# Clearing a 177 MB scratch table by 3 large DMAs instead of 88 small ones, in a four-layer GNN kernel

## The reference

```python
h = jnp.maximum(_layernorm(x), 0.0)
x = x + _L0_gnn_ref(h, edge_index, ...)      # edge MLP, segment_max over dst
h = jnp.maximum(_layernorm(x), 0.0)
x = x + _L1_gnn_ref(h, src, dst, ...)        # GCN: segment_sum with degree norms
h = jnp.maximum(_layernorm(x), 0.0)
x = x + _L2_gnn_ref(h, ..., src, dst)        # two hops of mean aggregation
h = jnp.maximum(_layernorm(x), 0.0)
x = x + _L3_gnn_ref(h, edge_index, edge_weight, ...)
# L3: message = x[dst] * edge_weight; segment_sum(message, src); two products with weights
```

## Time and profile before

| | |
|---|---|
| median of 3 runs | 14147.0 us (14146.95 to 14180.07) |
| the profiled execution's own time | 14180.07 us |
| its span | 14178.3 us |
| PE busy | 7232.4 us, 51% |
| DVE busy | 9168.8 us, 65% |
| ACT busy | 5831.1 us, 41% |
| POOL busy | 7818.9 us, 55% |
| moved by DMA | 1969.50 MB, mean 139 GB/s |
| mean granted clock of PE | 0.71 |

### The profile page before, as it was taken

One profiled execution on the slowest core, in us unless ns is written; L12 is line 12 of the kernel. 1 busy time (PEld: TensorE's weight loads), 2 busy tenths in 40 slices (PEclk: granted clock), 3 DMA queues, 4 the chain that ended last, 5 costly groups with the idle time before them and its releaser, 6 DMA issues. The chain is left out here.

```text
span 14178.3 us, 285510 instructions
## 1 busy us (share of the span) xinstructions
PE 7232.4 (51%) x96792; PEld 5249.9 (37%) x96792; DVE 9168.8 (65%) x18447; ACT 5831.1 (41%) x10200; POOL 7818.9 (55%) x7194
## 2 busy tenths in 40 slices
PE   2266666666666655996999999400000000000356
PEld 1255555555555543554555555300000000000355
DVE  5388888888888885335333433565666666666575
ACT  0144444444444444774776677322222222222000
POOL 5677777777777753110111111577777777777200
PEclk9866667666666667997999899655555555555676
DMA  7333333333333335884787688322222222221585
GB/s 311 130 116 113 110 118 112 114 115 110 113 116 110 116 105 151 256 253 142 246 258 227 189 252 258 101 65 63 65 65 65 65 65 62 65 62 60 178 255 179
DMA packets 1268462, 1969.50 MB, mean 139 GB/s; under 512 B 256937, under 2 KB 987918, under 8 KB 1262785
## 3 DMA queue, kind: packets, MB, share of 16 engines
q1 hardware_dynamic: 861601, 1047.59, 24.1%
q10 hardware_dynamic: 174288, 612.09, 11.6%
q0 software_dynamic: 231664, 297.80, 7.9%
HBM read 1155.02 MB, written 815.55 MB: 139 GB/s over the span
## 5 line engine op out<-in xcount | busy, mean ns | idle before, releaser
L633 POOL DMA_INDIRECT RF<-tab_edge_b,idx x3125 | 3546.5, 1135 | 1038.9 <-issue 947.5
L1187 POOL DMA_INDIRECT records<-RF,idx x3125 | 3150.1, 1008 | 986.9 <-issue 986.9
L686 DVE TENSOR_TENSOR HM<-iota_b,eqw 128x2048 bf16<-128x2048 bf16 x2000 | 2202.7, 1101 | 354.8 <-PE bk L1867 198.1
L1746 ACT ACTIVATE X<-bk 128x392 uint8<-128x392 f32 x4000 | 1782.0, 495 | 1566.4 <-PE bk L1867 1548.8
L1867 PE MATMUL bk<-HM 128*64 128x98 bf16 x32000 | 1577.9, 246 | 1319.7 <-ACT X L1746 660.5
L1867 PE MATMUL kp<-HM,ident_b 128*64 128x98 bf16 x6250 | 281.5, 283 | 3804.1 <-DVEq L1649 3804.1
L884 POOL DMA_INDIRECT agg<-RF,lastT x372 | 519.2, 1396 | 2983.8 <-ACT RF L819 2892.8
L777 PE MATMUL tp<-HM,RF 128*64 128x512 bf16 x12276 | 2107.9, 380 | 5.6 <-issue 4.2
L1867 PEld LDWEIGHTS bk<-HM 128*64 128x64 bf16 x32000 | 1235.3, 133 | 1665.4 <-issue 1582.9
L1867 PEld LDWEIGHTS kp<-HM,ident_b 128*64 128x64 bf16 x6250 | 261.5, 168 | 3825.0 <-issue 3825.0
L783 PE MATMUL om<-HM,RF 128*64 128x512 bf16 x6138 | 1429.5, 379 | 0.0
(11 more groups left out here) (364 smaller groups left out, 15278.6 us busy)
## 6 DMA issues: line engine op xcount, KB each, us to landing
dst_f<-counts SPq DMA_DIRECT2D x465, 512.0 KB, 4.4
RF<-first_rows SPq DMA_DIRECT2D x250, 800.0 KB
counts<-X ACTq DMA_DIRECT2D x250, 784.0 KB
records<-RF ACTq DMA_DIRECT2D x88, 1960.0 KB
RF<-records SPq DMA_DIRECT2D x220, 784.0 KB, 4.5
crow<-counts SPq DMA_DIRECT2D x279, 512.0 KB
first_rows<-RF ACTq DMA_DIRECT2D x25, 4000.0 KB, 49.4
edge_rows<-RF ACTq DMA_DIRECT2D x125, 800.0 KB, 7.9
```

The lines of the kernel that those rows point to most:

```text
L633: e.indirect_dma_start(out=ring[:, r, j, :], out_offset=None, in_=table[:, :], in_offset=bass.IndirectOffsetOnAxis(ap=idx[:, r, j:j + 1], ...
L686: return e.tensor_tensor(to[:, 0:n, :].rearrange("p k (q h) -> p k q h", h=2), iota_b[:, 0:m].rearrange("p (q h) -> p q h", h=2).unsqueeze ...
L1187: e.indirect_dma_start(out=records[:, :], out_offset=bass.IndirectOffsetOnAxis(ap=idx2[:, r, j:j + 1], axis=0), in_=msgs[MSG_OF[r]][:, j, ...
L1746: e.activation(staged[u].rearrange("p (r k) -> p r k", k=P)[:, :, k:k + 4], bk[s % 2][:, 0:4 * TILES].rearrange("p (k r) -> p r k", k=4), ...
```

## The change

The clears leave the loop over groups. ACT issues three instead, each ahead of one dense stage, of 206, 206 and 204 rows per partition. Source, destination and size of a row are the same, as is the sum. SP and POOL wait for 48 instead of 16 x 88.

```diff
-CLEARS, CLEAR_ROWS, CLEAR_COLS = 88, 7, 560
+CLEAR_COLS, CLEAR_ROWS = 560, 616
...
                 if later:
                     rows_out(g - 1, 1 - u)
-
-                if not isinstance(g, int) or g > (0 if l == 0 else 1):
-                    e.dma_start(records_flat.rearrange("(p c w) -> p c w", p=P, w=CLEAR_COLS)
-                                [:, bass.ds(g * CLEAR_ROWS + (-1, 28, 57)[l] * CLEAR_ROWS, CLEAR_ROWS), :],
-                                zero_tile[:, 0:CLEAR_COLS].unsqueeze(1).broadcast_to([P, CLEAR_ROWS, CLEAR_COLS]))\
-                        .then_inc(sem("records_zeroed"), 16)
-            e.wait_ge(sem("zero_tile"), 1)
             groups(e, group)
...
-            e.wait_ge(sem("records_zeroed"), 16 * CLEARS)
+            e.wait_ge(sem("records_zeroed"), 48)
...
             for l, name, norm in ((1, "gcn", 2), (2, "hop1", None), (3, "hop2", 3)):
+                e.wait_ge(sem("zero_tile"), 1)
+                part = slice((l - 1) * 206, min(l * 206, CLEAR_ROWS))
+                e.dma_start(records_flat.rearrange("(p c w) -> p c w", p=P, w=CLEAR_COLS)[:, part, :],
+                            zero_tile[:, 0:CLEAR_COLS].unsqueeze(1).broadcast_to([P, part.stop - part.start, CLEAR_COLS]))\
+                    .then_inc(sem("records_zeroed"), 16)
                 dense_scalar(e, l - 1)
```

More of the change, by code:

```diff
@@ L63, in build @@
     assert N <= ROWS and E == P * LANE and LANE == K * R * ITERS and BLOCKS == R * ITERS
-    assert (E + TILES * (SG - 1)) // SG <= GMAX and UNITS % 4 == 0 and GMAX * SG * RW == P * CLEARS * CLEAR_ROWS * CLEAR_COLS
+    assert (E + TILES * (SG - 1)) // SG <= GMAX and UNITS % 4 == 0 and GMAX * SG * RW == P * CLEAR_ROWS * CLEAR_COLS
     ctx = ExitStack()
```

## The result

The changed kernel takes 14385.55 us (median of 4 runs, 14375.16 to 14405.51), the kernel before 14148.15 us beside it: a ratio of 1.0163, 95% interval 1.0148 to 1.0177, or 237 us slower. The forecast was 14540, slower by 393 us, with a range from 14400. The profiled execution of after has a span of 14385.3 us.

A forecast was written before the change was run, and what follows sets the result against it. PE's matmuls were taken to bound the dense stages, with counts loads as the supply that must keep up. Loss 145 less 15 covered, 130 us per stage, three stages 390, on 14147 gave 14540 us; range 14400 to 14660.

The forecast's parts named there:

- What is removed is worth 0: Dense stages: 88 small clears cost ACT 33 us of issue, but nobody waited, so removing them gains 0.
- Does ACT stand still?: ACT's issue of each big clear: taken as 0 delay; upper bound 160 us per stage.
- Can SP get past?: SP's counts loads behind ACT's big clear: not shut out; if false, about 160 us per stage.
- One packet of each queue in turn: DMA engines during a big clear: alternate packets whatever their size, so SP's loads get 32% of what moves.
- 1.2 us per SP packet: Three SP stores beside ACT's 32,000 B packets, 27 packets in all: read as evidence that queues take turns.
- The rate while both run: Clear and loads together in a dense stage: 300 GB/s, so 290 us of overlap and 145 us lost.
- The bounds: Rate of clear and loads together: 328 GB/s gives 315 us in all, 282 GB/s gives 445.
- The cover: Start of each dense stage: 7 us from the clear's head start plus 8 of full buffers, 15 off the loss.
- The clock: PE's granted clock in the starved stretch: a fall to half adds only 0 to 15 us per stage.
- exclusive transfer: Dense stages: big clear shuts out loads or ACT stands until nearly drained; 14580 to 14630 us, chance 0.21.
- hidden: Dense stages: loads get all they ask for, the clear takes the rest; 14147 us, chance 0.09.
- faster: ACT in dense stages: per-clear costs vanish, 33 to about 42 us; 14105 to 14114 us, chance 0.04.

The follow-up runs named there:

- e3: Changed kernel with each stage's clear issued as 29 or 30 DMAs of 7 rows back to back; 414.3 us over the kernel before, ratio 1.0214.
- e7: Kernel before with clears of 28 rows after every fourth group (22 DMAs) instead of 7 after every group; 141.0 us over before, ratio 1.0075.
- e2: Changed kernel with clear rows of 3920 B instead of 2240 B, same bytes; 285.0 us over the kernel before, ratio 1.0147.
- e8: Changed kernel with clear rows of 560 B instead of 2240 B; 232.1 us over the kernel before, ratio 1.0123.

## Why the prediction was right or wrong

*What is removed is worth 0*: right on the chip of the forecast, to about 1 us: a stage with 30 clears of 7 rows takes 1074.9 us there, one without any 1073.9 (e3, another chip). On the third chip of the experiments they cost some 4 us a stage.

*Does ACT stand still?* Right, twice: one DMA of 1,648 packets per engine is issued in 0.41 us; 29 of 57 hold ACT for 143.68 us.

*Can SP get past?* Right, but late: the first packet of a load comes at 5465, 4.6 us after its issue, and up to there the clear runs alone.

*One packet of each queue in turn*: right. The counts of packets show it at 2240 and 3920 B directly (23,350 to 23,355 and 11,545 to 11,543), and nearly so at 1120 B (1.06 to one). With 560 B rows it holds only where both queues have packets; over a longer stretch it is 1.58 to one. The Trainium skill's rule ("DMA: Bandwidth & Descriptors", section "Queues, rings and completion order"), that each engine goes round its queues at packet granularity, agrees with the first three row sizes, and with the fourth in the window of 4 us. The prediction came to the rule by less sure a way: its 1.2 us per SP packet is 1.32 by its own figures (35.75 us for 27), and leaves some 3 us for issue and landing. The counts of that trace would have shown it at once.

*The rate while both run, 282 to 308, "I take 300"*: this step failed. It is 401 to 404 GB/s, over 200 us of each stage. Put into the same sum, 26,368 pairs of 3,295 B at 403 GB/s take 216 us instead of 290 (measured: 212.6 to 214.8), and the loss is 216 - 145 = 71 us instead of 145. The rows read for it were real, but they are edges. e7 shows such an edge by itself: 285 GB/s for 1 us just before the loads join, then 395 and more. In before the first load packets come at 5567.3, and in 5568 to 5569 and 5569 to 5570 the two queues have

```profile
q10 hardware_dynamic: 86, 0.19, 76.9%
q1 hardware_dynamic: 87, 0.09, 25.7%
```

```profile
q1 hardware_dynamic: 166, 0.17, 49.2%
q10 hardware_dynamic: 66, 0.11, 52.1%
```

In the second the clear is already over on part of the engines. In the first they do take turns, at 282 GB/s instead of 403; why so slowly is not shown. The bounds had the same fault: 282 to 328 are bounds of a transient. With loads alone at 386 and a clear alone at 385 in the same rows, nothing but those few microseconds spoke for a lower rate of both.

*The cover, 7 + 8 = 15 us per stage*: this term was off too, in the other direction. From the windows of after, 84.9 MB move in the 212 us from 5454 to 5666; less 59.1 of the clear that leaves 25.8 MB, or 3.94 groups, 134 us of PE's work. The loads are short by 78 us, and the first stage is 74.6 us longer, so the cover is about 3 us per clear. An estimate in the same way for the others (3.5 us alone at 365 GB/s, then the clear at 0.68 of 403): 14 rows leave the loads 6.8 us short and cost 3.3, 28 rows 11.6 and 6.7, 7 rows 4.4 and about 0. Cost as the shortfall less 3 to 5 us, once per clear, fits all four; it is an estimate, made after the runs. By it 7 rows per group lie just below the edge. Why four full buffers, 11 us of PE's work, cover no more than this is not shown.

The two errors work against each other. By the forecast's own sum, the right rate alone gives 3 x (71 - 15) = 168 us, or 14315, which is 70 us under the measured time; the wrong cover hid part of the wrong rate. With both put right it is 3 x 68 = 204 us, against 227 in the three stages. Most of the rest is the start: the 71 us count both as running from the first packet, but for 12 us only the clear moved, and with these the shortfall is 78.

*The clock*: granted 0.76 in the first 10 us in which both run and 0.88 to 0.95 after, lower than before's 1.00. As expected it does not add: the shortfall of the loads explains the first stage to 4 us.

*Rivals*: an exclusive transfer was not seen in the changed kernel (e3 produces one by another way); hidden and faster did not come. The 2 us that the prediction quotes for the faster case from the Trainium skill ("DMA: Bandwidth & Descriptors", section "Anatomy of one DMA — SWDGE (gpsimd) path") are given there for DMAs that POOL issues; the clears are ACT's.

## What to carry to other kernels

Here a background transfer was harmless only while its burst was shorter than what the buffers of the loads beside it covered. So cut it so that it runs dry before they do, or issue it where nobody loads. If it must run beside them, the size of its rows sets its share, since each queue gets one packet per turn; but rows that are too small are slow by themselves. To forecast such a share, count the packets of each queue in a window, and read the rate of both from a long overlap; a few microseconds at the edge of one are no steady state.

## What the runs showed of the hardware that was not expected

- A store with 2240 B rows and a load stream together moved 403 GB/s, more than that store alone at 375 and the loads alone at 386.
- Store rows of one size moved alone: 560 B 171 GB/s, 1120 B 316, 2240 B 375, 3920 B 414 (e2, 9126 to 9130). The DMA share was 1.22 at the first and 1.01 to 1.03 at the others.
- A load that is issued while only a clear runs starts late. In before one was issued at 5562.84, 0.8 us behind a clear of 7 rows, and its first packet came at 5567.3; in e7 9175.38 and 9179.9; in after 5460.41 and 5465.0, 8 us into the clear: 4.5 to 4.6 us each. In e8, with 560 B rows, it took 7.1 us (9125.74 to 9132.8). Without a clear it took 1.0 us (after, 5709.78 to 5710.8). What the load waits for was not tried. The issues of before and of after:

```profile
5562.84 0.38 SPq L749 DMA_DIRECT2D dst_f<-counts  x1
```

```profile
5460.41 0.37 SPq L749 DMA_DIRECT2D HM<-counts  x1
```

- The same kernel takes 14,148 us on one chip and 18,828 to 18,982 on three others. The dense part is within 14 us; the time goes in the stages of gathers and scatters. In 2000 to 4000 us POOL waits 1022.3 us there for SP's small load `cix`, and the first dense stage begins at 8978.8 instead of 5464.2 (before again). Why such a load is slow on those chips stays open.
